# A graph network kernel: edge block 30 sorted too, sum and count matmuls merged, counts zeroed by ScalarE, halves added first, block 0 reordered

## What is computed

```python
m = gelu(h_E @ m0_w + m0_b)            # 16384 x 512 -> 256
m = gelu(m @ m1_w + m1_b)
m = gelu(m @ m2_w + m2_b)
dh = segment_sum(m, src_idx, 512) / 30
h = layer_norm(h_V + dh, ln1_g, ln1_b)
d = gelu(h @ d0_w + d0_b); d = gelu(d @ d1_w + d1_b); d = d @ d2_w + d2_b
out = layer_norm(h + d, ln2_g, ln2_b)
```

## Time and profile before

| what | value |
| --- | --- |
| runs | 600.34, 602.75, 602.92 us; median 602.75 |
| profiled execution | 600.45 us, its span 598.6 us |
| TensorE busy | 579.4 us (97%) |
| VectorE busy | 460.3 us (77%) |
| ScalarE busy | 366.2 us (61%) |
| edge stage | until about 436 us |
| node MLP | about 438 to 504 us |
| attention and the rest | about 504 us to the end |

### The profile page before, as it was taken

One profiled execution on the slowest core, in us unless ns is written; L12 is line 12 of the kernel. 1 busy time (PEld: TensorE's weight loads), 2 busy tenths in 40 slices (PEclk: granted clock), 3 DMA queues, 4 the chain that ended last, 5 costly groups with the idle time before them and its releaser, 6 DMA issues.

```text
span 598.6 us, 9053 instructions
## 1 busy us (share of the span) xinstructions
PE 579.4 (97%) x3195; PEld 497.2 (83%) x3195; DVE 460.3 (77%) x792; ACT 366.2 (61%) x557; POOL 228.4 (38%) x208
## 2 busy tenths in 40 slices
PE   7999999999999999999999999999989999998895
PEld 5778888898988898888898888899978889677763
DVE  4777577878778887888998789879776566877667
ACT  6677687777777777777776777767275443221242
POOL 3065567565666544555454555430000010200011
PEclk9999999999999999999999999999999999999999
DMA  8254388395566637556563875223171304000000
GB/s 291 107 166 136 138 287 233 125 286 179 160 202 213 183 106 244 153 159 203 162 208 105 326 240 173 90 81 90 45 316 72 149 1 141 0 2 0 1 0 35
DMA packets 34507, 86.89 MB, mean 145 GB/s; under 512 B 3873, under 2 KB 23201, under 8 KB 29857
## 3 DMA queue, kind: packets, MB, share of 16 engines
q1 hardware_dynamic: 27264, 67.09, 35.6%
q0 software_dynamic: 6912, 19.10, 8.5%
q10 hardware_dynamic: 288, 0.13, 0.1%
HBM read 66.69 MB, written 19.62 MB: 144 GB/s over the span
## 4 chain that ended last, share of the span: by engine, by line
PE 88%; DVE 6%; ACT 2%; issue 2%; DMA 1%; POOL 0%; POOLq 0%; SPq 0%; DVEq 0%; ACTq 0%
PE ps L1304 27%; PE ps L1356 10%; PE ps L1515 7%; PE ps L1338 5%; PE ps L1362 5%; PE ps L1334 5%; PE ps L1333 5%; PE ps L1481 4%; PE ps L1406 3%; PE ps L1408 3%; PE ps L1410 3%; PE ps L1557 2%; PE ps L1527 2%; PE ps L1546 1%; PE ps L1608 1%
## 5 line engine op out<-in xcount | busy, mean ns | idle before, releaser
L475 POOL DMA_INDIRECT sorted_rows<-m,place x120 | 167.7, 1397 | 153.3 <-ACT m L538 125.6
L521 ACT ACTIVATE m_hi<-ps,cols 128x512 fp32r<-128x512 f32 x128 | 88.4, 691 | 73.2 <-PE ps L1304 40.9
L836 DVE TENSOR_TENSOR m_lo<-m_out,m_hi 128x512 fp32r<-128x512 f32 x128 | 88.6, 693 | 53.7 <-ACT m_out L523 47.5
L1304 PE MATMUL ps<-x_hi,w_hi 128*128 128x512 f32 x248 | 96.9, 391 | 0.0
L1304 PE MATMUL ps<-x_lo,w_hi 128*128 128x512 f32 x248 | 96.9, 391 | 0.0
L1304 PE MATMUL ps<-x_hi,w_lo 128*128 128x512 f32 x248 | 96.6, 390 | 0.0
L523 ACT ACTIVATE m_out<-ps,cols 128x512 f32<-128x512 f32 x128 | 88.0, 688 | 0.0
L718 DVE TENSOR_TENSOR x_lo<-x_raw,x_hi 128x1024 fp32r<-128x1024 f32 x62 | 73.1, 1220 | 5.4 <-ACT x_hi L515 4.9
L1356 PE MATMUL ps<-w_lo,m_hi 128*128 128x256 f32 x256 | 64.2, 283 | 0.0
L538 ACT ACTIVATE m<-m_in 128x512 f32<-128x512 f32 x64 | 39.5, 635 | 40.2 <-DVE m_in L849 40.2
L1356 PE MATMUL ps<-w_hi,m_hi 128*128 128x256 f32 x256 | 64.0, 282 | 0.0
(11 more groups left out here) (226 smaller groups left out, 1200.1 us busy)
## 6 DMA issues: line engine op xcount, KB each, us to landing
x_raw<-in_edges_dram SPq DMA_DIRECT2D x31, 1024.0 KB
sorted_raw<-sorted_rows SPq DMA_DIRECT2D x24, 647.5 KB
sorted_raw<-sorted_rows SPq DMA_DIRECT2D x6, 518.0 KB
d_w<-in_d_dram SPq DMA_DIRECT2D x3, 1024.0 KB, 4.7
d_w<-in_d_dram SPq DMA_DIRECT2D x1, 3072.0 KB, 9.8
rows<-in_rows_dram SPq DMA_DIRECT2D x1, 2176.0 KB, 8.4
sorted_rows<-m,place POOLq DMA_INDIRECT x120
w_raw<-in_w_dram SPq DMA_DIRECT2D x4, 256.0 KB, 5.8
```

The source lines that it names most:

```text
L475: pool.indirect_dma_start(out=sorted_d, out_offset=bass.IndirectOffsetOnAxis(ap=place[:, at:at + 1], axis=0), in_=m2[:, b % 2, t], in_offs ...
L521: nc.scalar.activation(out_hi[:, m], ps[:, bank], ACT.Gelu, bias=col(bias, m)).then_inc(hi_signal, 1)
L836: nc.vector.tensor_tensor(lo[:, m], m_out[:, m], hi[:, m].bitcast(F32), ALU.subtract).then_inc(done, 1)
L1304: last = nc.tensor.matmul(out, left, right, start=(k == 0 and i == 0), stop=(k == KE - 1 and i == 2))
```

## The change

It has five parts.

1. Block 30 is sorted as well. `SORT_BLOCKS` is seven sorts of 4 and one of 3, the last one has blocks 28 to 30, and there are 31 chunks, 0 to 30. Only block 31 is direct. Chunk 27 has four tiles, chunks 28 to 30 five.
2. Sum and count of a group share one bank (banks 4 to 7), and `sorted_hi` and `pack_hot` one buffer (`hi_pack`). A tile is one matmul of 512 columns and one of 256.
3. The counts are no longer cleared by PE after a copy. ACT writes the two times two fields back times zero (`counts_zero`).
4. The order around the seam is a new one, and the norm waits for the last sorted chunk (`sorted_summed`) instead of the direct sums. `d1_w` is loaded in five single pieces and a rest of three.
5. In block 0, `rest_x(2, 1)` stands after `rest_0(1, 1)`. In the attention, DVE adds the two halves of one product (`halves_added`), and PE adds up four parts of it instead of eight.

```diff
-DIRECT = (NBLK - 2, NBLK - 1)
-SORT_BLOCKS = (4,) * 6 + (3,) * 2
+DIRECT = (NBLK - 1,)
+SORT_BLOCKS = (4,) * 7 + (3,)
...
-D1_FIRST = KD - 6
+D1_FIRST = KD - 3
-COUNT_AFTER = (6, 13, 20, NQ - 6)
+COUNT_AFTER = (6, 13, 20, 24)
+EARLY = 16 * (2 + D1_FIRST)
...
+        group_both = ps[:, SUM:SUM + NC]
+        group_sum, group_cnt = group_both[:, :, 0:H], group_both[:, :, H:]
...  (SP)
-                    sp.dma_start(d1_w[:, 0:D1_FIRST].rearrange("p a b -> p (a b)"), d1_d[:, 0:D1_FIRST * D]).then_inc(early_loaded, 16)
+                if b >= NBLK - 6 and b - (NBLK - 6) < D1_FIRST:
+                    k = b - (NBLK - 6)
+                    sp.dma_start(d1_w[:, k], d1_d[:, k * D:(k + 1) * D]).then_inc(early_loaded, 16)
...  (ACT)
+            def counts_zero(s):
+                act.wait_ge(count_out, 2 * s + 2)
+                for r in range(2):
+                    fields = group_cnt[:, 2 * r:2 * r + 2]
+                    nc.scalar.activation(fields, fields, ACT.Copy, scale=0.0).then_inc(count_zero, 1)
...
                 if b in COUNTS_OUT_AT:
                     counts_out(COUNTS_OUT_AT.index(b))
+                    counts_zero(COUNTS_OUT_AT.index(b))
                 gelu_1(b, 0)
...
+                if b == NBLK - 2:
+                    counts_out(COUNTS - 2)
                 gelu_2(b, 0)
...
-            round_sorted(NQ - 4)
-            counts_out(COUNTS - 2)
+            counts_zero(COUNTS - 2)
+            round_sorted(NQ - 5)
             gelu_1(NBLK - 1, 0)
             gelu_1(NBLK - 1, 1)
+            round_sorted(NQ - 4)
+            gelu_2(NBLK - 1, 0)
+            gelu_2(NBLK - 1, 1)
             for q in range(NQ - 3, NQ):
                 round_sorted(q)
-            gelu_2(NBLK - 1, 0)
-            gelu_2(NBLK - 1, 1)
...  (DVE)
                     count_groups()
                     rest_x(2, 0)
-                    rest_x(2, 1)
...
                 rest_0(b + 1, 1)
+                if b == 0:
+                    rest_x(2, 1)
...
-            dve.wait_ge(direct_summed, 1)
-            dve.wait_ge(early_loaded, 48)
+            dve.wait_ge(sorted_summed, NQ)
+            dve.wait_ge(early_loaded, EARLY)
...
+            def halves_added(c, made):
+                dve.wait_ge(dve_step, made)
+                half = HEADS * H // 2
+                nc.vector.tensor_tensor(prod[c][:, 0:half], prod[c][:, 0:half], prod[c][:, half:],
+                                        ALU.add).then_inc(prod_ready, 1)
...
+            halves_added(0, out_made)
             for half in range(2):
...  (PE)
-                if q == 0 or q - 1 in COUNT_AFTER:
-                    if q:
-                        pe.wait_ge(count_out, 2 * COUNT_AFTER.index(q - 1) + 2)
-                    clear(CNT)
-                    clear(CNT + 1)
+                if q - 1 in COUNT_AFTER:
+                    pe.wait_ge(count_zero, 2 * COUNT_AFTER.index(q - 1) + 2)
...
-                    nc.tensor.matmul(group_sum[:, g], hot, sorted_hi[:, q % 2, t], start=False, stop=False,
+                    nc.tensor.matmul(group_both[:, g], hot, hi_pack[:, q % 2, t], start=False, stop=False,
                                      skip_group_check=True)
-                    nc.tensor.matmul(group_sum[:, g], hot, sorted_lo[:, q % 2, t], start=False, stop=True,
-                                     skip_group_check=True)
-                    last = nc.tensor.matmul(group_cnt[:, g], hot, pack_hot[:, q % 2, t], start=False, stop=True,
+                    last = nc.tensor.matmul(group_sum[:, g], hot, sorted_lo[:, q % 2, t], start=False, stop=True,
                                             skip_group_check=True)
...
+                if b == NBLK - 2:
+                    sum_sorted(b - LAG_SUM)
                 layer_2(b)
                 layer_0(b + 1, 1)
-                if b >= LAG_SUM:
+                if LAG_SUM <= b < NBLK - 2:
                     sum_sorted(b - LAG_SUM)
             layer_1(NBLK - 1)
+            sum_sorted(NQ - 6, late_groups[NQ - 6])
             sum_sorted(NQ - 5, late_groups[NQ - 5])
+            layer_2(NBLK - 1)
             sum_sorted(NQ - 4, late_groups[NQ - 4])
-            sum_direct(DIRECT[0])
+            sum_direct(NODE_HALF[0])
             sum_sorted(NQ - 3, late_groups[NQ - 3])
-            layer_2(NBLK - 1)
-            for q in (NQ - 2, NQ - 1):
-                sum_sorted(q, late_groups[q])
-            sum_direct(DIRECT[1])
+            sum_direct(NODE_HALF[1])
+            sum_sorted(NQ - 2, late_groups[NQ - 2])
+            sum_sorted(NQ - 1, late_groups[NQ - 1])
...
-            add_up(0, OUT_BANK[0])
+            add_up(0, OUT_BANK[0], HEADS // 2)
```

More of the change, by code:

```diff
@@ L972, in prepare @@
                     hot_dst(q, t)
+            def prepare(q):
+                hots(q)
                 rest_sorted(q)
+            prepare(NQ - 5)
+            rest_1(NBLK - 1, 0)
+            rest_1(NBLK - 1, 1)
             prepare(NQ - 4)
+            biased(NBLK - 1, 0)
+            biased(NBLK - 1, 1)
+            hots(NQ - 3)
             rest_direct(DIRECT[0], 0)
             rest_direct(DIRECT[0], 1)
-            rest_1(NBLK - 1, 0)
-            rest_1(NBLK - 1, 1)
-            for q in range(NQ - 3, NQ):
-                prepare(q)
-            biased(NBLK - 1, 0)
-            biased(NBLK - 1, 1)
-            rest_direct(DIRECT[1], 0)
-            rest_direct(DIRECT[1], 1)
+            rest_sorted(NQ - 3)
+            prepare(NQ - 2)
+            prepare(NQ - 1)
             steps = [0]
@@ L1075, in _ @@
                     last = nc.vector.bn_stats(stats[:, c], res[:, c])
+                    if c == NODE_HALF[1][0]:
+                        last.then_inc(sums_read, 1)
                 link(last)
@@ L1371, in rank_edges @@
                 own = flat[:, :, COLS_SORT - 1:]
-                nc.tensor.matmul(ps[:, CNT], all_ones[:], own, start=True, stop=True)
+                nc.tensor.matmul(ps[:, RANK], all_ones[:], own, start=True, stop=True)
                 for d in range(COLS_SORT):
-                    last = nc.tensor.matmul(ps[:, CNT + 1], all_ones[:] if d else before_me[:],
+                    last = nc.tensor.matmul(ps[:, RANK + 1], all_ones[:] if d else before_me[:],
                                             flat[:, :, COLS_SORT - 1 - d:2 * COLS_SORT - 1 - d], start=(d == 0),
@@ L1421, in sum_direct @@
                         if g == 0 and t % 2 == 0:
-                            pe.wait_ge(direct_split, 2 * i + t // 2 + 1)
-                        hot = direct_hot[:, i, t, g * P:(g + 1) * P]
-                        nc.tensor.matmul(group_sum[:, g], hot, direct_hi[i][:, t], start=False, stop=False, skip_group_check=True)
-                        nc.tensor.matmul(group_sum[:, g], hot, direct_lo[i][:, t], start=False, stop=True, skip_group_check=True)
-                        last = nc.tensor.matmul(group_cnt[:, g], hot, direct_pack[:, i, t], start=False, stop=True,
+                            pe.wait_ge(direct_split, t // 2 + 1)
@@ L1427, in sum_direct @@
+                        hot = direct_hot[:, 0, t, g * P:(g + 1) * P]
+                        nc.tensor.matmul(group_sum[:, g], hot, direct_hi[0][:, t], start=False, stop=False, skip_group_check=True)
+                        nc.tensor.matmul(group_sum[:, g], hot, direct_lo[0][:, t], start=False, stop=True, skip_group_check=True)
+                        last = nc.tensor.matmul(group_cnt[:, g], hot, direct_pack[:, 0, t], start=False, stop=True,
                                                 skip_group_check=True)
-                    if b == DIRECT[-1]:
-                        last.then_inc(group_summed, 1)
@@ L1430, in sum_direct @@
-                nc.tensor.matmul(ps[:, 1, 0:P], no_weight[:], iota[:, 0:P], start=True, stop=True).then_inc(direct_summed, 1)
+                last.then_inc(direct_summed, 1)
             def keep_warm(products, bank):
```

64 lines of the change are left out of this document (31 added, 33 removed).

## The result

| kernel | median of its runs (us) | range | ratio to the kernel before, 95% interval |
|---|---|---|---|
| before | 600.43 | 599.97 to 602.92 | 1 |
| changed | 607.75 | 607.11 to 608.09 | 1.0108, 1.0089 to 1.0126 |

The change makes the kernel 1.1% slower. I had forecast 599.5 with a range up to 603.0. The profiled execution of the changed kernel took 607.83 with a span of 605.7; the one of before has a span of 598.6, so the two traces differ by 7.1 and are good for finding where it went.

A forecast was written before the change was run, and what follows sets the result against it. PE, busy 97% of the span, was taken as the bound, with exceptions such as the seam; -1.1 - 1.2 - 1.3 + 2.5 - 0.9 = -2.0 gave 598.4 (profiled) or 600.7 (median), named 599.5, range 596.5 to 603.

The forecast's parts named there:

- block 0's order: Block 0 on DVE: moving the second x_lo half behind m_lo shortens PE's waits, gain 1.1, bounds 0.8 and 1.14.
- clears, three pairs: Chunks 7, 14 and 21: PE's clears go, ACT zeroes the banks instead, 0.44 a pair, gain 1.3.
- merges: Sums up to chunk 23: a tile costs 0.347 instead of 0.358, 114 tiles, gain 1.2.
- seam: Between edge and node stage, block 30 sorted: DVE's chain starts the norm at 435.6 against 433.09, loss 2.5, bounds 1.8 and 5.
- after the norm: Node stage: transposes follow after the same 3.4, later steps keep their distances, so no cost.
- added halves: Attention: PE adds half as many products, saving 1.8, DVE gets one addition of 1.21; gain 0.9, bounds 0.8 and 1.8.
- DVE waits 0.4: Seam: reload of chunk 28 usable at 420.5, DVE ready at 420.1, so a wait of 0.4.
- The direct matmuls lie in the shadow of this: Seam: PE's direct sums are hidden behind DVE's work on the last chunks and add no time.
- C: Rival: block 30's round trip through DRAM is late in the seam, slower, 603 to 606; chance 0.10.
- D: Rival: merged matmul costs two, or ACT's zeroing makes PE wait; -0.8 or +1.6, 599.7 to 602; chance 0.14.
- B: Rival: seam costs under 1.8 since reloads land before DVE asks; -2.7 to -3.3, 599.4 on the median; chance 0.26.
- A: The forecast itself as a case: total change of -1 to -3; chance 0.50.

The follow-up runs named there:

- e6_mended: Changed kernel with direct subtractions first, chunk 27's hot matrices ahead of m_lo, group numbers loaded two blocks earlier, 14 + 4 zero products in PE's waits: 601.12, ratio 0.9996.
- e4_hots27: Changed kernel, but VectorE makes the hot matrices of chunk 27 before the two m_lo subtractions of block 31: 605.63, ratio 1.0062.
- e3_direct_first: Changed kernel, but VectorE makes the two direct subtractions of block 31 before the hot matrices of chunk 28: 604.29, ratio 1.0040.
- e2_warm: Changed kernel with 22, 14 and 4 useless multiplications by zero weights put into three waits of TensorE: 604.40, ratio 1.0047.
- e8_before_idle: Kernel before, with two 128x1024 additions on VectorE ahead of the first half's normalized rows, so that TensorE idles before the first transposes: 604.53, ratio 1.0068.
- e7_wide_then_narrow: Changed kernel, but each chunk's sum does its five 512-wide products first and its five 256-wide ones after: 606.16 (one run).
- e1_parts_only: Changed kernel with blocks 30 and 31 unsorted and the seam of before restored, chunk 24's group numbers loaded a block earlier: 599.35, ratio 0.9952 to before.

## Why the prediction was wrong

| term | forecast | measured in the trace | |
|---|---|---|---|
| block 0's order | -1.1 | -1.14 | right |
| clears, three pairs | -1.3 | -1.32 | right: 0.44 at blocks 14, 21 and 28 |
| merges | -1.2 | -0.23 | mis-sized |
| seam | +2.5 | +7.03 | the step that failed |
| after the norm | 0 | +2.97 | missing |
| added halves | -0.9 | -0.76 | right |
| start of this execution | | +0.56 | not the change |

**The seam, +2.5.** Step by step, with 2.13 added to the changed kernel's times so that they stand on the clock of before, as the forecast did:

- DVE's m_in of block 31 was to end at 420.1 and ended at 421.3. Of the 1.2, 0.9 is layer_2 of block 30: in front of chunk 24's sum the sequencer of PE loads two sets of group numbers, and PE's wait for "issue" is 0.7. I had counted the sum that moved (1.74) and not the register loads that moved with it. e6_mended removes it. The other 0.3 is not explained.
- "DVE waits 0.4" for reload 28 was 2.80. The gate was 11.15 instead of 8.78, and the reload took 4.41 to its use instead of 4.07. I took 8.78 from a block in which VectorE's fp32 subtractions lay differently. The spread of a scatter that I had put in the bounds, 0.96 to 2.40 by the earlier trace rows, was no scatter of chance: it follows VectorE. Behind the layer of block 31 VectorE has no pause left, so the fourth scatter was at 3.87, outside the bounds. e4_hots27 showed it.
- "The direct matmuls lie in the shadow of this" was wrong as well. In the text I had put the direct subtractions behind the hot matrices of chunk 28, and so behind the reload, and did not ask what PE does meanwhile. It idled 5.69, then did 24 direct products and the sum of chunk 28 at 0.62 of its clock, so that VectorE waited 0.94 for it before chunk 30 where 0.3 was forecast, and the last hand-over was 0.25 longer. e3_direct_first showed it: the norm starts 2.1 earlier, and VectorE no longer waits for reload 28. In that order the late reload costs nothing (34.01 from block 30's third layer to the norm, and 34.00 in e6_mended with the faster scatter), so this step of the chain is the largest.
- With all of it mended, in e6_mended, the seam still costs 3.6 and not 2.5. There VectorE waits 0.62 and 0.35 for ScalarE ahead of the direct subtractions, a hand-over that my chain did not have, where I had put 0.4 for the reload.

**After the norm, 0.** I wrote that PE "now idles; the transposes follow after the same 3.4", and that everything behind keeps its distance. The transposes did follow after 3.38. But I priced an idle time of TensorE by its length alone, though a clock row with a 9 in every slice says only what happens without such an idle time. No row of before had one of 3 us in it but the start. e2_warm and e8_before_idle show the price.

**Merges, -1.2.** The two durations, 0.228 and 0.119, were right, and e7_wide_then_narrow gets most of the gain that follows from them (1.0 of 1.2). They came from stretches of one width. By turns, wide and narrow cost 0.007 a tile more than in groups, and that is two thirds of the 0.011 that there was to gain. The Trainium skill's rule, which I had set aside there ("TensorE: Matmul & The Clock Gate", section on the back-to-back issue gap: N/2.4 plus 2.5 ns, so 2.5 ns saved a merge), gives an estimate of 0.3 for the 114 tiles; the trace has 0.23 for the 110 up to block 29. That fits the size, though not the cause: with the products regrouped the gain is 1.0, and the rows of one width have about 12 to 14 ns beyond the streamed columns.

**The rivals.** C was the right one in kind: the round trip of block 30, slower, "scatters that queue". It had 0.10, and its 603 to 606 still lies under the 607.75 measured. Its condition, 5 us more in the seam to lose 0.5%, was in fact 4.5 more, and the clock and the missing merge gain did the rest. Its reason was wrong: the scatters do not queue behind reload 27, they get longer beside VectorE's fp32 subtractions. Half of D came true, too: a part that doesn't do what it says, in the merges. ScalarE's zeroing held nobody up in the loop, and PE waited for count_zero nowhere. Of the signs that I named for being wrong, "DVE idle for the reload of chunk 28 by more than 1" is the one that came. In attention the reduction waited for nothing and the stage gained 0.76, as B's and A's sums had it.

My chance of slower, 0.10, was too low for a change that puts a wait of DRAM length in front of an engine that I myself had described as having no slack. A chain of ten hand-overs, in which an early one only waits for the next and a late one moves the end, has its errors mostly on one side.

## What to carry to other kernels

When a change opens an idle time on a TensorE that was busy throughout, price it at its length plus a stretch at the lower clock, here 1.7 for 2.7 us and between 1.4 and 3.0 for 3.4 us, or put other work (even useless products) into it. Ask for each wait that is new in an engine's queue what stands behind it without needing it, and move that ahead: three lines were worth about 3 us, and with them a transfer that was 1.2 late cost nothing. Before the work of one block is sent a longer way to save another engine some products, compare with leaving it where it is and taking only the parts that shorten the loop: those alone made this kernel 0.65% faster.

## What the hardware did that I had not expected

- A scatter issued by GpSimd took 0.96 to 1.08 in the changed kernel where VectorE had less than 0.5 us of fp32 subtractions or additions with two inputs beside it, and up to 3.87 under 2.5 us of them; the reload behind it was later by the same amount (9.98 against 11.15 when the order on VectorE changed).
- A 512-wide and a 256-wide product by turns cost 0.007 a pair more than five wide ones and then five narrow ones (0.79 over 23 sums, 110 pairs).
- Group numbers loaded into TensorE's registers just ahead of the product that uses them cost 0.9 to 1.4 in the one place where two sets stood together (15.18 to 15.64 for that block); loaded a block or two earlier, nothing (14.27 and 14.28, in e1_parts_only and e6_mended).
- After idle times of 5.7 us, and of 3.4 with 1.2 right behind it, TensorE's granted clock was 0.62 and 0.57 in the windows 425 to 430 and 445 to 450, in which it worked without a pause, and 1.00 in the windows after them. After one of 2.7 with 1.2 behind it (e8_before_idle) it was 0.66 in the window 440 to 445, and behind waits of 1.2 to 1.6 (e3_direct_first, 420 to 430) it stayed at 1.00.
